# Paired projections and one shared row window for tent-sampled half strips

## The reference, cut to what matters

```python
om = conv2d(x, w_om) + b_om                 # offsets y and x for 9 taps, in C1 and C2 also a mask
py = row + k // 3 - 1 + off_y[k]            # for each of the 9 taps k, at each pixel
px = col + k % 3 - 1 + off_x[k]
samp = bilinear(x, py, px) * sigmoid(mask)  # four corners, zero outside the image
out = einsum("bckhw,ock->bohw", samp, w)    # the projection: 9 taps x 32 channels -> 32 channels
```

## Time and profile before

| | us |
|---|---|
| median of three runs | 7570.2 |
| profiled execution, its own time | 7556.77 |
| its span, first to last instruction | 7555.0 |
| L0 of pair 0, first to last of 24 steady d steps | 110 to 551 |
| L0 of pair 1 with C1 of pair 0 | 704 to 1680 |
| L0 of pairs 2 and 3 with C1 of pairs 1 and 2 | 1975 to 2868, 3057 to 3892 |
| C1 of pair 3 (g and c in turns) | 4270 to 5068 |
| C2 | 5068 to 7555 |

### The profile page before, as it was taken

How to read it: one execution, slowest core, us unless ns; L and a number is a source line. 1 busy time by engine, 2 the same in 40 slices (tenths; PEclk the granted TensorE clock), 3 DMA queues, 4 the chain that set the end, 5 groups by cost and what they waited for, 6 DMA issues and landing times. The chain is left out here.

```text
span 7555.0 us, 126024 instructions
## 1 busy us (share of the span) xinstructions
PE 6270.8 (83%) x47672; PEld 4785.5 (63%) x47672; DVE 4889.0 (65%) x11222; ACT 2182.7 (29%) x3358; POOL 4986.7 (66%) x4909
## 2 busy tenths in 40 slices
PE   7985766664888887788887798879998998998997
PEld 6874555553666665566665454447776776776775
DVE  6885666664777675677775445546776766676665
ACT  1112122221222222222222222224443443443442
POOL 0006777776767673777674566676777777777776
PEclk9996877885989998889898788879998998998998
DMA  4222333333333332333332222223333333332332
GB/s 136 93 84 87 92 91 94 92 89 92 104 88 98 86 87 69 88 93 94 97 90 59 67 67 65 62 74 86 90 86 87 91 88 77 99 90 76 97 85 72
DMA packets 366236, 653.67 MB, mean 87 GB/s; under 512 B 113896, under 2 KB 272488, under 8 KB 357736
## 3 DMA queue, kind: packets, MB, share of 16 engines
q0 software_dynamic: 156672, 321.18, 16.8%
q1 hardware_dynamic: 209000, 324.67, 14.0%
HBM read 599.42 MB, written 46.07 MB: 85 GB/s over the span
## 5 line engine op out<-in xcount | busy, mean ns | idle before, releaser
L831 POOL DMA_INDIRECT G<-table,IDX x4896 | 4972.6, 1016 | 2522.0 <-issue 2174.7
L1345 ACT ACTIVATE SAMP<-RED 96x384 f32<-96x384 f32 x1216 | 590.8, 486 | 4507.6 <-PE RED L1048 1521.9
L1981 DVE TENSOR_TENSOR ARENA<-ARENA 128x288 f32<-128x288 f32 x3744 | 1451.0, 452 | 302.8 <-PE RED L1048 288.0
L1048 PE MATMUL RED<-IDENT,ARENA 128*96 128x128 f32 x11232 | 1443.2, 287 | 199.0 <-DVE ARENA L1981 199.0
L1048 PEld LDWEIGHTS RED<-IDENT,ARENA 128*96 128x96 f32 x11232 | 1294.5, 133 | 316.8 <-issue 286.3
L1838 DVE TENSOR_TENSOR G<-G,W 128x1152 f32<-128x1152 f32 x476 | 645.9, 1357 | 540.1 <-DMA G<-table,IDX 532.1
L1153 PE MATMUL BTP<-PAD,ARENA 80*128 x2304 | 756.3, 452 | 73.4 <-DVE ARENA L1831 37.9
L1019 PE MATMUL OUT<-SAMP,WDCN 96*32 96x128 f32 x4992 | 740.6, 297 | 77.6 <-ACT SAMP L1345 77.0
L1033 PE MATMUL RED<-IDENT,SUM 128*96 128x128 f32 x1056 | 223.6, 330 | 678.6 <-DVE SUM L1852 678.5
L991 PE MATMUL OFFC<-PAD,ARENA 128*54 128x128 f32 (+1 forms) x10944 | 744.7, 295 | 27.1 <-ACT PAD L1254 15.3
L991 PEld LDWEIGHTS OFFC<-PAD,ARENA 128*54 128x54 f32 (+1 forms) x10944 | 664.2, 134 | 92.9 <-issue 71.0
(11 more groups left out here) (199 smaller groups left out, 6192.4 us busy)
## 6 DMA issues: line engine op xcount, KB each, us to landing
ARENA<-wtab SPq DMA_DIRECT2D x208, 800.0 KB
G<-table,IDX POOLq DMA_INDIRECT x4896
ARENA<-xo SPq DMA_DIRECT2D x96, 720.0 KB
table<-TB SPq DMA_DIRECT2D x64, 384.0 KB, 2.5
X<-xo SPq DMA_DIRECT2D x64, 360.0 KB, 3.5
X<-x SPq DMA_DIRECT2D x2, 3200.0 KB, 22.4
out<-X SPq DMA_DIRECT2D x20, 320.0 KB
wtab<-TB SPq DMA_DIRECT2D x16, 384.0 KB, 2.9
```

Of the source, the lines that this page charges most:

```text
L831: pool.indirect_dma_start(G[:, b, k, :], None, tables[seg.table], bass.IndirectOffsetOnAxis(ap=IDX[:, q, b * TAPS + k:b * TAPS + k + 1], a ...
L1048: last = nc.tensor.matmul(RED[b % 2][0:TPG * C, gr * 128:(gr + 1) * 128], PROD[gr][:, sft, :], IDENT[:, :], start=(sft == 0), stop=(sft == ...
L1345: nc.scalar.activation(SAMP[:, x], RED[x][0:TPG * C, 0:GROUPS * 128].rearrange("p (g n) -> p g n", g=GROUPS), ACT.Copy).then_inc(z.samp_re ...
L1981: last = nc.vector.tensor_tensor(out=PROD[gr][:, :, j * C:(j + 1) * C].rearrange("p (dy dx) c -> p dy dx c", dy=3), in0=win[:, gr:gr + 3, ...
```

## The change

Projections: `project_images` takes both images of one half tt at once and issues their six matmuls in turns, image 0 and image 1, which go to different column groups of the array. It is issued after unit 2 (in a d step in the middle of unit 2) and at the end of the step; in a c step at the end alone. The semaphore still rises once for each image.

Half strips: both rows of a half now use one window of source rows. A tap is one matmul of 128 columns of x tents (both rows) by 15 rows x 32 channels = 480 columns. In the y tents row r = 1 gets an offset that is larger by one (BELOW_ROW1 is 6 for the first row and 7 for the second). WY1 falls from 16 to 15, so the sum over rows has 15 transposing matmuls for a group instead of 16. For pair 3 the c steps take the rows 32 to 63 instead of 16 to 47; their number stays.

```diff
--- before.py
+++ after.py
@@ -48,8 +48,8 @@
 MIXED = ("gd" * 4 + "gdd") * 2 + "gd"
 MIXED_C = ("gddgddgc" * 2) * 3 + "gdd"
 WBUILD = range(0, 5), range(5, 9)
-C1_ROWS = {1: (32, 48), 2: (32, 48), 3: (16, 48)}
-WY1, BELOW1 = 16, 7
+C1_ROWS = {1: (32, 48), 2: (32, 48), 3: (32, 64)}
+WY1, BELOW1 = 15, 6
 TAPW1 = WY1 * C
 
 L0, C1, C2 = 0, 1, 2
@@ -155,7 +155,8 @@
         PRODS1 = {p: [t.rearrange("p (w c) -> p w c", w=WY1) for t in (alone if p == PAIRS - 1 else shared)] for p in C1_ROWS}
         SMAX1 = lent(6528, IDXS)
         SNEG1 = lent(6564, IDXS)
-        CONST1 = lent(6600, 2 + WY1)
+        CONST1 = lent(6600, 3 + WY1)
+        BELOW_ROW1 = CONST1[:, 2 + WY1:3 + WY1]
         NEGP1, ONE1, IOTA1 = CONST1[0:W, 0:1], CONST1[0:W, 1:2], CONST1[:, 2:2 + WY1]
         COLUMN1 = X[96:98, 0, 0:256]
         STEPS1 = X[96:98, 0, 256:256 + SCOLS]
@@ -1006,19 +1007,19 @@
                         pe.wait_ge(seg.z.prep_v, PREP * (n - 1) + 1)
                     on.turn_offsets(seg, t, q, n, md)
 
-                def project(step, b):
-                    on.project_unit(step.seg, step.u, step.po, b, step.v + b, b % 2)
-
-                def project_unit(seg, u, po, b, v, x):
+                def project_images(step, tt):
+                    seg = step.seg
                     z = seg.z
-                    pe.wait_ge(z.samp_ready, v + 3)
-                    if b == 0:
-                        pe.wait_ge(z.out_read, u + 2 if z is main and seg.s == C2 else u + 1)
-                    at = seg.p % 2 * R2 + b % 2 * C
+                    pe.wait_ge(z.samp_ready, step.v + 2 * tt + 1 + 3)
+                    if tt == 0:
+                        pe.wait_ge(z.out_read, step.u + 2 if z is main and seg.s == C2 else step.u + 1)
                     for gr in range(GROUPS):
-                        last = nc.tensor.matmul(out_slot(seg, po)[at:at + C, b // 2 * 128:(b // 2 + 1) * 128], WDCN[:, seg.s, gr, :],
-                                                SAMP[:, x, gr, :], start=(gr == 0), stop=(gr == GROUPS - 1))
-                    last.then_inc(z.projected, 1)
+                        for im in range(2):
+                            at = seg.p % 2 * R2 + im * C
+                            last = nc.tensor.matmul(out_slot(seg, step.po)[at:at + C, tt * 128:(tt + 1) * 128], WDCN[:, seg.s, gr, :],
+                                                    SAMP[:, im, gr, :], start=(gr == 0), stop=(gr == GROUPS - 1))
+                            if gr == GROUPS - 1:
+                                last.then_inc(z.projected, 1)
 
                 def consume(step):
                     z, m, prep = step.seg.z, step.i, step.prep
@@ -1034,9 +1035,9 @@
                                                        SUM[:, b % 2, TPG * gr:TPG * (gr + 1), :].rearrange("p k c -> p (k c)"),
                                                        IDENT[:, :])
                         last.then_inc(z.reduced, 1)
-                        if b:
-                            on.project(step, b - 1)
-                    on.project(step, UNITS - 1)
+                        if b == 2:
+                            on.project_images(step, 0)
+                    on.project_images(step, 1)
 
                 def consume_dense(step):
                     z, prep = step.seg.z, step.prep
@@ -1049,13 +1050,13 @@
                                                         PROD[gr][:, sft, :], IDENT[:, :],
                                                         start=(sft == 0), stop=(sft == 8), is_transpose=True)
                             last.then_inc(prod_used, 1)
-                            if b and gr == 1:
-                                on.project(step, b - 1)
+                            if b == 2 and gr == 1:
+                                on.project_images(step, 0)
                         if prep and b == 0:
                             on.convolve(*prep)
                         if prep and b == 1:
                             on.turn_offsets(*prep)
-                    on.project(step, UNITS - 1)
+                    on.project_images(step, 1)
 
                 def reduce_half(step, im, gr):
                     if gr == 0:
@@ -1084,23 +1085,20 @@
                                 c = 18 * h + 9 * im + k
                                 if c > 1:
                                     pe.wait_ge(weighted1, c - 1)
-                                for r in range(2):
-                                    row = strip_row(seg, t // 2) + t % 2 * 2 + r + k // 3 - 1 - BELOW1 - r0
-                                    last = nc.tensor.matmul(BTP[c % 2][64 * r:64 * r + 64, 0:TAPW1], TX1[p][im][:, k, r * SCOLS:(r + 1) * SCOLS],
-                                                            XT1[p][:, im, row:row + WY1, :].rearrange("p w c -> p (w c)"), start=True, stop=True)
-                                last.then_inc(taps1, 1)
+                                row = strip_row(seg, t // 2) + t % 2 * 2 + k // 3 - 1 - BELOW1 - r0
+                                nc.tensor.matmul(BTP[c % 2][:, 0:TAPW1], TX1[p][im][:, k, :],
+                                                 XT1[p][:, im, row:row + WY1, :].rearrange("p w c -> p (w c)"),
+                                                 start=True, stop=True).then_inc(taps1, 1)
                             if gr:
                                 on.reduce_half(step, im, gr - 1)
                             elif im:
                                 on.reduce_half(step, 0, GROUPS - 1)
-                            if im and gr == 1:
-                                on.project(step, 0)
                         if prep and im == 0:
                             on.convolve(*prep)
                     on.reduce_half(step, 1, GROUPS - 1)
                     if prep:
                         on.turn_offsets(*prep)
-                    on.project(step, 1)
+                    on.project_images(step, 0)
 
                 def dense_done(u):
                     pass
@@ -1563,12 +1561,14 @@
                     for w in range(WY1):
                         nc.vector.memset(IOTA1[:, w:w + 1], float(w))
                     nc.vector.memset(COLUMN1[:, 128:256], 0.0)
+                    nc.vector.tensor_copy(BELOW_ROW1, BASE_Y[:, 0:1])
                     for c in range(TC):
                         nc.vector.tensor_scalar(STEPS1[:, c:SCOLS:TC], BASE_X[96:98, 0:SCOLS // TC * TAPS:TAPS], float(c), None, ALU.add)
                     last = nc.vector.scalar_tensor_tensor(out=NEGP1, in0=BASE_Y[0:W, 0:1], scalar=-float(TC), in1=BASE_X[0:W, 0:1],
                                                           op0=ALU.mult, op1=ALU.subtract)
                     last.then_inc(const1_ready, 1)
                     dve.wait_ge(const1_ready, 1)
+                    nc.vector.tensor_scalar(BELOW_ROW1, BELOW_ROW1, float(SCOLS // TC), float(BELOW1), ALU.is_ge, ALU.add)
                     first, second = IDENT[96:98, 96:97], IDENT[96:98, 97:98]
                     nc.vector.tensor_scalar(COLUMN1[:, 0:128].rearrange("p (r c) -> p r c", r=2),
                                             STEPS1.unsqueeze(1).to_broadcast([2, 2, SCOLS]), first, second, ALU.mult, ALU.add)
@@ -1613,7 +1613,7 @@
                     dve.wait_ge(mask1, cs + 1)
                     after(0)
                     nc.vector.tensor_scalar(FLAT[:, :].rearrange("p (tt im k) -> p tt im k", tt=2, im=2), turned(seg, t)[:, :, :, 0:2 * TAPS:2],
-                                            float(BELOW1), None, ALU.add).then_inc(prep_v, 1)
+                                            BELOW_ROW1, None, ALU.add).then_inc(prep_v, 1)
                     after(1)
                     nc.vector.tensor_tensor(out=SMAX1, in0=SMAX1, in1=FLAT[:, :], op=ALU.max).then_inc(range1_ready, 1)
                     nc.vector.scalar_tensor_tensor(out=SNEG1, in0=FLAT[:, :], scalar=-1.0, in1=SNEG1, op0=ALU.mult, op1=ALU.max).then_inc(range1_ready, 1)
```

## The result

The kernel after takes 7427.5 us (median of 4 runs, 7424.5 to 7459.6), the kernel before 7568.65 us beside it. The ratio is 0.982, with an interval of 0.981 to 0.984. The forecast was 7345 us, a ratio of 0.970: of 223 us of gain 141 came. The time lies just inside the upper end of the range (7430); the ratio, applied to the 7570.2 us that the forecast started from, gives 7436, just outside it. The profiled execution took 7424.5 us, 132.2 less than the one before, where the sum of terms said 228.

The account below looks back on a forecast made before the run. PE was taken to bound L0 of pair 0 and the stages of pairs 1 to 3, gathers pair 0's stage. Terms 45 + 8 + 57 + 62 + 56 = 228 us gave 7329; median offset and small waits made it 7345, range 7315 to 7430.

Parts of the forecast that it names:

- L0 of pair 0, 45 us: First layer of pair 0: 26 d steps fall from 18.39 to 16.65 us as projection blocks go, 45 us gained.
- the row of C2: C2's trace: both images in turns, next work 0.78 us later, so a block of two costs what one costs.
- the estimate from the factor of the Trainium skill: Projections: 1.6 times for two column tiles, so a pair would take 0.95 us and the gain be about 12% smaller.
- A group of the c step: Taps and sums of one group in a c step: 4.24 instead of 4.84 us, 0.6 us less.
- the rival without overlap: Projection pairs don't overlap beside L0's sums, only c steps gain, about 60 us: 7510 us, chance 0.05.
- Pair 1, 57 us: Pair 1's stage: 13 dd and 8 c give 68 us, 11 go to waits for gathers, 57 us gained.
- I carried the tiles one after the other with POOL's own durations of the trace: Stages with gathers: tile-by-tile estimate of gains lost to gather waits, keeping the earlier trace's call durations; 11 us in pair 1.
- denser steps could lengthen them: Gathers take over: POOL's calls, 0.94 to 1.4 us, lengthen; waits of 29 us become 75: 7391 us, chance 0.14.
- the gain that a dd and a c pass on to the g behind them: Work before a g step: gdd gives 2.7 us, a c 3.9 us, or 4.35 us with a `prep`.
- Pairs 2 and 3, 62 and 56 us: Stages of pairs 2 and 3: 68 less 7 gives 62 us (rounded), and 67 less 11 gives 56 us.
- the joined block: c step: the projection block joined with the other image's saves 0.77 us of the step's 3.9 us gain.
- Pair 0, 8 us: Pair 0's stage, held by gathers: only four dd places and the tail before the normalization give something, 8 us.

Follow-up runs that it names:

- two pauses: Kernel after plus two DVE waits in d steps (behind the X update, before the second part of the tents): 7397.7 us, ratio 0.975 to the kernel before.
- turns with pauses: Kernel before with only the projections in turns, plus two DVE waits in d steps (behind X update, before second part of tents): 7479.6 us, 0.988 of before.
- rows alone: Kernel before with only the shared 15-row window and pair 3's rows 32 to 63, projections unchanged: 7496.0 us, 0.9915 of before.
- turns alone: Kernel before with only the projections of two images in turns, half strips unchanged: 7580.4 us, 0.9987 of before.

## Why the prediction was wrong

**L0 of pair 0, 45 us: right.** The step is 16.6 us for 16.65, the term 45.0. The pair overlaps as the row of C2 said; by the estimate from the factor of the Trainium skill it would have been 0.95 us, and it is 0.78. (That estimate would have taken a fifth from the gain of a d step, 2 x 0.17 of 1.73 us; the 12% in the prediction are too few for that step.) A group of the c step was right to 0.1 us. PEclk of L0 stayed at 1.00, C2 kept its length, and no step took the form of the rival without overlap.

**Pair 1, 57 us: wrong, 3 came.** The step that failed first is the sentence "I carried the tiles one after the other with POOL's own durations of the trace". These durations were no property of POOL. They hung on DVE's waits, which I listed in the earlier trace rows and counted only as spare time of DVE; the turns use up exactly them. I had the effect as a rival ("denser steps could lengthen them"), but with a call of up to 1.4 us as the worst, where 4.45 us was measured, and with 75 us of waits at 7391. In pair 1's stage 43.8 us of DVE's waits for gathers stood where I had 11. The trace of before already had calls of over 1.6 us, 114 of them, and a timeline of POOL held against DVE's would have shown what they ended with. The two pauses give 27 of the missing 54 us of pair 1 back, and 28 to 58 us of the whole.

**The other half of pair 1 is the g steps, and open.** With the pauses DVE waits for no gather there, and the steps still give 30 us and not the 68 that I had before the waits. So a second step failed, the gain that a dd and a c pass on to the g behind them (2.7 and some 4 us). Pair 1's g steps are still 30 us longer than before and nearly the same in turns with pauses (30) but not in rows alone (7), so it comes with the turns. From the end of one g to the end of the next over a dd it is 54.2 us before and 52.6 with both and pauses (means of the six between a d and a dd), 1.7 less and not 2.7; over c, g and dd it is 106.3 and 103.3, 3.0 less and not 6.6. The rows of the g step show two things. DVE has less of a lead at its start: in the earlier trace rows the g step's first sums start at once, and after they wait 0.54 us, and 2.02 instead of 1.44 for the second. I had held that all of the first d's gain and half of the second's lie before DVE's last product, so that they pass on whole. And the convolution in the g step runs at the lower clock more often: of the 49 convolutions of pair 1's stage 10 took over 3 us before and 17 after, in pair 0's stage 9 of 52 and 26. The mean granted clock of pair 1's stage went from 0.90 to 0.84. PE is idle for longer between the d steps, which I had looked for in L0 alone. No run here tells how much each of the two costs.

**Pairs 2 and 3, 62 and 56 us: 42 each.** In pair 2 DVE waits 6.0 us for gathers and the pauses change 1 us, so its missing 20 us are of the open kind: its g steps grew by 24. In pair 3 the c steps gained 51 us together, where the prediction had 67, and the g steps between them took 9 back. Here I was wrong on who gives it: 0.77 us of each c step were to come from the joined block, and the turns alone gave nothing there (7 us less in the c steps, 7 more in the g steps).

**Pair 0, 8 us: 3 lost.** Its d steps gained 49 us and its g steps lost 52, held by gathers as I had said; but the direction of the small rest was not mine to know. The turns alone lost 24 there, with the same code in that stage. I take it that which calls happen to begin ahead of a long run is a matter of phase, and that this moves the stage by some 20 us; this was not tested.
